# A DLRM tower with cross layers: ten embedding gathers spread otherwise over the four tiles of a group

## What is computed

```
e = stack(tbl_f[ids[:, f]] for f in range(39))         # (1024, 39, 16)
x0 = xk = e
for W in (f0, f1, f2):                                  # three cross layers of 128 features
    z = einsum('bfd,bgd->bfgd', x0, xk).reshape(b, f*g, d)
    xk = einsum('bpd,pm->bmd', z, W)
    outs.append(xk)
z = concatenate(outs, axis=1).sum(-1)                   # (1024, 384)
h = relu(concatenate([z, dense_ctx], 1) @ W_top1 + b_top1)
h = relu(h @ W_top2 + b_top2)
y = h @ W_top3
```

## Time and profile before

| | us |
|---|---|
| median of three runs | 1338.92 |
| lowest and highest | 1338.18, 1340.23 |
| span of the profiled execution | 1331.2 |
| TensorE busy | 1271.8 |
| GpSimd busy | 1046.5 |
| VectorE busy | 973.0 |
| ScalarE busy | 733.6 |

### The profile page before, as it was taken

The page is one execution under the profiler, slowest core; times in us unless marked ns, Lnnn a source line. Parts: engine busy times, 40 slices in busy tenths (PEclk is TensorE's granted clock), DMA queues, the critical chain, the costliest instruction groups (busy, mean ns, idle before and its releaser), DMA issues.

```text
span 1331.2 us, 25256 instructions
## 1 busy us (share of the span) xinstructions
PE 1271.8 (96%) x5493; PEld 951.9 (72%) x5493; DVE 973.0 (73%) x3253; ACT 733.6 (55%) x2422; POOL 1046.5 (79%) x937
## 2 busy tenths in 40 slices
PE   0799999999999999999999999999999999999999
PEld 0477777777787777777777776877777777877765
DVE  4677786888758787777868887578876778688740
ACT  4365564656546565555646565456655566466641
POOL 6568888788878898688887988779887888876540
PEclk9999999999999999999999999999999999999999
DMA  7632221222211222122212222122222221221000
GB/s 169 172 89 66 67 58 33 61 55 65 63 46 47 61 66 60 54 65 66 52 37 59 56 65 63 29 59 66 60 60 59 66 57 41 55 56 55 2 1 1
DMA packets 121771, 78.48 MB, mean 59 GB/s; under 512 B 77437, under 2 KB 89827, under 8 KB 121653
## 3 DMA queue, kind: packets, MB, share of 16 engines
q1 hardware_dynamic: 106124, 73.45, 19.7%
q0 software_dynamic: 10240, 2.64, 2.6%
q10 hardware_dynamic: 5288, 1.32, 0.5%
HBM read 18.50 MB, written 2.63 MB: 16 GB/s over the span
## 4 chain that ended last, share of the span: by engine, by line
PE 66%; DVE 15%; issue 8%; POOL 4%; ACT 2%; DMA 2%; SPq 1%; DVEq 1%; ACTq 0%; POOLq 0%
PE ps L516 15%; PE ps L520 14%; PE ps L517 14%; PE ps L495 13%; DVE terms L835 11%; PE ps L540 5%; DVE prods L807 3%; PE ps L530 3%; POOL terms L433 3%; PE ps L599 2%; ACT terms L686 2%; PE ps L609 1%; POOL x_in L405 1%; DMA dense_rows<-in_dense_ctx 1%; DMA w<-in_f 1%
## 5 line engine op out<-in xcount | busy, mean ns | idle before, releaser
L835 DVE SCALAR_TENSOR_TENSOR terms<-ps,x_scal,terms 128x128 f32<-128x128 f32 x2944 | 807.0, 347 | 280.9 <-ACT terms L686 171.4
L686 ACT ACTIVATE terms<-ps,x_scal 128x128 f32<-128x128 f32 x2048 | 584.0, 376 | 412.1 <-PE ps L520 267.3
L433 POOL TENSOR_TENSOR terms<-terms 128x1024 f32<-128x1024 f32 (+2 forms) x384 | 566.1, 1474 | 106.0 <-DVE terms L835 85.0
L516 PE MATMUL ps<-w_high,x_high 128*128 128x512 f32 (+1 forms) x1280 | 590.0, 461 | 25.0 <-DVE terms L835 16.8
L520 PE MATMUL ps<-w_high,x_low 128*128 128x512 f32 (+1 forms) x1280 | 497.3, 389 | 0.0
L517 PE MATMUL ps<-w_low,x_high 128*128 128x512 f32 (+1 forms) x1280 | 495.8, 387 | 0.0
L405 POOL DMA_INDIRECT x_in<-in_tables,row_at x320 | 303.7, 949 | 89.8 <-issue 69.8
L516 PEld LDWEIGHTS ps<-w_high,x_high 128*128 128x128 f32 x1280 | 240.6, 188 | 154.3 <-DVE terms L835 65.2
L517 PEld LDWEIGHTS ps<-w_low,x_high 128*128 128x128 f32 x1280 | 241.6, 189 | 67.0 <-issue 28.1
L520 PEld LDWEIGHTS ps<-w_high,x_low 128*128 128x128 f32 x1280 | 240.3, 188 | 49.5
L495 PE MATMUL ps<-prods,w 117*128 117x512 f32 x262 | 135.1, 601 | 9.2 <-DVE prods L807 9.2
(11 more groups left out here) (48 smaller groups left out, 416.2 us busy)
## 6 DMA issues: line engine op xcount, KB each, us to landing
prods<-x_cols SPq DMA_DIRECT2D x190, 234.0 KB
x_cols<-x_rows SPq DMA_DIRECT2D x93, 78.0 KB
x_first<-x_cols SPq DMA_DIRECT2D x93, 78.0 KB
x_in<-in_tables,row_at POOLq DMA_INDIRECT x320, 2.4
x_diag<-x_scal SPq DMA_DIRECT2D x256, 9.8 KB
s<-in_f SPq DMA_DIRECT2D x3, 832.0 KB, 11.5
x_rows<-x_in SPq DMA_DIRECT2D x31, 80.0 KB, 2.4
wt<-in_W_top SPq DMA_DIRECT2D x1, 768.0 KB, 13.1
```

What stands on the lines that cost most here:

```text
L433: nc.gpsimd.tensor_tensor(t[:, 0:n], t[:, 0:n], t[:, n:2 * n], ALU.add).then_inc(s_tree, 1)
L516: nc.tensor.matmul(y, x1_high[:, par, at:at + P], high, start=True, stop=False)
L686: op = nc.scalar.activation(terms[:, u % 2, FB * ACT_BANKS.index(q) + i, :], ps[:, (BANKS * u + q) % RING, i * G:(i + 1) * G], ACT.Copy, s ...
L835: nc.vector.scalar_tensor_tensor(out=acc, in0=y, scalar=x0, in1=acc, op0=ALU.mult, op1=ALU.add).then_inc(s_mac, 1)
```

## The change

The ten gathers of a group were shared out as 2, 3, 2 and 3 to the places t0 to t3 (from 10t/4 to 10(t+1)/4, rounded down). Now a table gives them as 1, 2, 4 and 3. Their number, their order among themselves, and every other instruction stay. The last batch, which gathers in its group 0 alone, has the same shares.

```diff
--- before.py
+++ after.py
@@ -89,6 +89,7 @@
 FOUR = P // SAMPLES
 FETCHES = -(-F // FOUR)
 AHEAD = 3
+GATHERS = (0, 1, 3, 7, 10)
 TREE = (8, 4, 2)
 
 
@@ -439,7 +440,7 @@
             def gathers(u):
 
                 t = u % TILES
-                return range(FETCHES * t // TILES, FETCHES * (t + 1) // TILES)
+                return range(GATHERS[t], GATHERS[t + 1])
 
             prologue()
             with pool.Fori(0, NBATCH - 1) as bt:
```

## The result

The changed kernel took 1349.80 us (median of 4 runs, 1348.12 to 1356.45), against 1339.09 for the kernel before beside it: a ratio of 1.0092, 95% interval 1.0075 to 1.0108. Both are slower; the first is outside the predicted range, the second at its upper end. And the kernel has a property that the one before has not: its time varies by 8 to 10 us between the executions of a session, where that of the kernel before stays within 2.1 to 4.5.

What follows compares the result with a forecast made beforehand. GpSimd, saturated for most of a batch, was taken as the bound. Five batch ends at -0.38 us, one at +1.51 and one at -0.56 gave -0.95: 1338.92 to some 1338.0 us, range 1334.3 to 1342.5.

Steps and rivals of the forecast that it cites:

- What bounds the kernel: GpSimd is saturated from t3 of a batch's group 0 to the batch's end, holding ScalarE through X.
- X: The end of GpSimd's last add of a tile (L437); ScalarE may overwrite terms only after that of two tiles before.
- The price of a gather: On GpSimd between its waits: one gather costs 1.26 us, four in a row before the next T 4.94.
- gathers cost by place: Slower rival: t2's two extra gathers each wait out a VectorE operation, 0.28 us, up to 16 us; chance 0.03.
- Entry: Loss in group 0 of a batch: T of t3 starts 0.74 us late, and all groups behind are late.
- T: GpSimd's first tree add of a tile (128x1024).
- Exit: End of a batch: ScalarE's first scale of t0 comes 1.12 us earlier, less 0.74 us: 0.38 us a batch gained.
- Holes: GpSimd idle before gathers 114 and 224 stays with them; the first costs 1.89 us, the second 1.32.
- Rival B: Slower: at batch ends X of t3 holds ScalarE's first scale of t1; 1344 to 1346 us, chance 0.10.
- The base: Profiled span 1331.2 us against a median of 1338.92: 7.7 us taken as outside the span, untouched by the change.
- The range: Predicted time 1334.3 to 1342.5 us, taking in a faster rival and the forecast's own 1336.5 to 1340.5.

Runs made afterwards that it cites:

- its repeat: The kernel before, run again with no edit in a second session: median 1338.21 us of 10 runs, ratio 1.0001.
- second trace: The changed kernel, run again with no edit in a second session: median 1341.76 us of 10 runs, ratio 1.0034 against the kernel before.

## Why the prediction was wrong

**What bounds the kernel: right.** GpSimd's saturation from t3 of group 0 to the end of the batch, and the exit through X, are borne out by the five kernels that took gathers off that part or out of the way of X of t2: the batch fell from 155.5 to 154.5, 153.4 and 153.0, where TensorE leads.

**The price of a gather: the step that failed.** "One gather costs GpSimd 1.26 us" is right (1.25 in the slot of four). That this is all it costs was not. The move made a row of four, during which TensorE's increments arrive up to 3 us late, and in this slot they are the first banks of t0. That is 9.05 us of the trace's 10.8. Nothing in the trace of before showed it: its loop has no row of four, and none of its increments is late behind a row of three either, where in its repeat they are, by 0.6 us. But the case "gathers cost by place" was priced with VectorE's operations only, given a chance of 0.03, and its test (gathers longer in the slot of four) looked at the wrong engine: they take 0.94 to 0.96 us there, as everywhere. The Trainium skill's rule of that place (page "SBUF — State Buffer", section "SBUF: two separate sides") is not what happened: by it the descriptor writing would have waited, and the gathers' rows show no wait: what waited were the increments of TensorE.

**Entry: right.** 4.95 against 4.94, no idle before T of t3, and 0.74 to 0.87 between the ordinary batches with four and with three.

**Exit: right, a little too high.** 0.20 (155.35) or 0.33 us (155.22, second trace) a batch, against 0.38. Without the entry loss 1.06 against 1.12.

**Holes: right in place, wrong in size.** I took over the 1.89 us surplus of a hole before a slot's second gather. Before a first one the surplus is 2.89 - 0.21 = 2.68. The first hole's batch cost 2.82 and the second's 2.00, where 1.89 and 1.32 were in the sum. Together that is 1.6 us, a sixth as much as the late starts.

**Rival B: real, but not here.** In the changed kernel X of t3 doesn't lead; with 2.52 us on it, it costs 0.8 a batch.

**The base: wrong, without effect.** Not 7.7 us lie outside the span but 1.8: 1350.79 less 1349.0 in the profiled execution of the changed kernel, 1328.88 less 1327.1 in another kernel's. The profiled execution of the kernel before was one with a short prologue (TensorE's first tile of the second layer at 44.6 us, in its repeat at 48.6), and with the 1.8 us it would have taken 1333.0, below every listed time of that kernel. A span of 1331.2 against a median of 1338.9 should have raised the question how well that one execution stands for the others; it didn't for the increments.

**The range** left out the tail that it should have had for a row longer than any the trace showed: a cost that no row bounds from above.

## What to carry to other kernels

Make no row of work longer than the trace has already shown, or ask what else runs while it is carried out: two changes that each gain 0.7% (here 2, 3, 2, 3 to 1, 3, 3, 3 or to 2, 2, 3, 3) can lose when put together, because the slot passes a length. Where one engine's work is periodic and saturated in a part of the period only, put what can be moved into the part in which it idles; here that gave 1.3%. Take a second trace of the kernel before, and compare: here the first, on which every row of the prediction rests, was 4.5 us shorter than its repeat and had no late increment at all. When two executions of one kernel differ by more than its neighbours' do, look for an event that only some groups suffer, and at which group it is paid.

## What the chip showed that I had not expected

- Increments by TensorE were recorded and acted on late while a row of indirect gathers, issued at a pitch of 1.25 us, was under way: by up to 3.1 us behind four or six in a row, in bunches 50 ns apart. Behind four the bunches came 1.9 to 2.7 us after the start of the last gather, behind six 2.2 to 2.8. Behind rows of three the increments were 0.6 us late in the repeat of the kernel before, one at a time, and up to 1.7 us, mostly in bunches of two, in others; behind its rows of two 0.1 to 0.2. Four gathers split two and two by an add of 2.4 us held none.
- What holds them isn't shown. Between 254.5 and 256.9 us in the trace of the changed kernel other semaphores' records are sparse too, and increments by DMAs stand bunched with the late ones. The first trace of the kernel before is the only one of the thirteen in which no record of these increments is missing (the others have 1082 to 1134 for 1280 banks), and the only one in which none is late. The repeat of the same kernel lacks as many records as the changed kernel does, and has late ones.
- One possibility that no run here tests: the Trainium skill, page "NOTIFIC — the notification-queue block", section "7.1 Overflow: three behaviours, one of which stalls the engine", says that the block's internal pipeline pushes back on its sources rather than lose a record. If event records did that here, the late increments would belong to executions that are recorded. Whether an execution without such records is slowed by a row of four isn't shown.
- A hole of 1.40 to 2.93 us stands before the 114th and the 224th indirect gather of every kernel in this case, 110 apart, whether 320 or 262 are issued, and it is the longer the earlier the gather stands in its slot.
